# Splitting one expert weight late: w1 stays float32 on chip and is split per block, attention splits w2 alone

## The reference, cut to what matters

```python
x = x + tanh(g_xattn) * xattn(layernorm(x), ctx, ctx)        # 16 heads of 64, context of 64 rows
xt = layernorm(x)                                            # (4096, 256)
w_topk, sel = top_k(xt @ gate_w.T, 2); w_topk = softmax(w_topk)
h = silu(einsum('td,edf->tef', xt, w1))                      # w1 (8, 256, 1024)
y = einsum('tef,efd->ted', h, w2)                            # w2 (8, 1024, 256)
x = x + tanh(g_ffn) * einsum('ted,te->td', y, combine)
```

## Time and profile before

| | |
|---|---|
| median of 3 runs | 850.42 us (848.83 to 853.76) |
| profiled execution, first to last instruction | 848.8 us |
| TensorE, VectorE busy | 769.0 us (91%), 661.1 us (78%) |
| ScalarE, GpSimd busy | 409.8 us (48%), 472.4 us (56%) |
| bytes moved by DMA | 92.52 MB, mean 109 GB/s |

### The profile page before, as it was taken

How to read it: one execution, slowest core, us unless ns; L and a number is a source line. 1 busy time by engine, 2 the same in 40 slices (tenths; PEclk the granted TensorE clock), 3 DMA queues, 4 the chain that set the end, 5 groups by cost and what they waited for, 6 DMA issues and landing times. The chain is left out here.

```text
span 848.8 us, 23770 instructions
## 1 busy us (share of the span) xinstructions
PE 769.0 (91%) x8130; PEld 623.5 (73%) x8131; DVE 661.1 (78%) x1330; ACT 409.8 (48%) x767; POOL 472.4 (56%) x446
## 2 busy tenths in 40 slices
PE   3978998988988888998789999999999999999993
PEld 2645665665655656665578999899999999999993
DVE  7878999999999999999855867766666666666661
ACT  3765776675757667575324444333333333333321
POOL 3434765786868678686633464844444444444442
PEclk9988999999999999999989999999999999999998
DMA  7404061533416153342167786432233332233321
GB/s 237 185 1 149 16 209 51 196 122 144 147 65 230 68 200 99 137 157 93 68 214 212 220 237 159 113 57 45 48 47 46 50 50 46 48 47 46 52 33 19
DMA packets 48837, 92.52 MB, mean 109 GB/s; under 512 B 4921, under 2 KB 32578, under 8 KB 48770
## 3 DMA queue, kind: packets, MB, share of 16 engines
q1 hardware_dynamic: 25730, 64.78, 22.6%
q0 software_dynamic: 13392, 18.03, 12.4%
q10 hardware_dynamic: 9648, 8.85, 3.9%
HBM read 53.69 MB, written 37.95 MB: 108 GB/s over the span
## 5 line engine op out<-in xcount | busy, mean ns | idle before, releaser
L1402 PE MATMUL h_ps<-bx_h,w_now 128*128 128x128 f16 x2272 | 196.1, 220 | 0.6 <-DVE w_now L1538 0.6
L1415 PE MATMUL pair_ps<-weights,ht_h 128*128 x1136 | 190.6, 273 | 0.9 <-ACT y L1481 0.6
L1402 PE MATMUL h_ps<-bx_l,w_now 128*128 128x128 f16 x1136 | 157.1, 220 | 0.0
L1402 PEld LDWEIGHTS h_ps<-bx_h,w_now 128*128 128x128 f16 x2272 | 155.1, 99 | 1.8 <-issue 1.0
L1645 POOL TENSOR_TENSOR wait_mark<-wait_mark 128x1 f32<-128x1 f32 x71 | 50.7, 714 | 189.1 <-ACT y L1481 144.5
L1415 PE MATMUL pair_ps<-weights,ht_l 128*128 x568 | 154.8, 273 | 0.0
L1474 ACT ACTIVATE hid<-h_ps 128x1024 f32<-128x1024 f32 x71 | 72.7, 1024 | 144.2 <-PE h_ps L1402 140.1
L1544 DVE CAST ht_h<-hid 128x1024 f16<-128x1024 f32 x71 | 49.5, 697 | 104.8 <-ACT hid L1474 104.8
L1215 POOL TENSOR_TENSOR r_l<-r,r_h 128x512 f16<-128x512 f32 x64 | 74.9, 1171 | 86.2 <-ACT r_h L804 83.5
L1646 POOL DMA_INDIRECT out<-y,meta x71 | 114.6, 1614 | 14.4 <-issue 6.1
L1415 PEld LDWEIGHTS pair_ps<-weights,ht_h 128*128 128x128 f16 x1136 | 110.2, 97 | 15.9 <-issue 1.7
(11 more groups left out here) (273 smaller groups left out, 1693.8 us busy)
## 6 DMA issues: line engine op xcount, KB each, us to landing
stage<-in_w SPq DMA_DIRECT2D x16, 1024.0 KB, 7.5
w_split<-split SPq DMA_DIRECT2D x14, 1024.0 KB, 5.9
weights<-w_split SPq DMA_DIRECT2D x14, 1024.0 KB
rows<-records ACTq DMA_DIRECT2D x67, 129.0 KB, 2.1
xin<-in_x SPq DMA_DIRECT2D x8, 512.0 KB, 4.2
x_even<-in_x SPq DMA_DIRECT2D x4, 512.0 KB, 3.6
x_odd<-in_x SPq DMA_DIRECT2D x4, 512.0 KB, 3.7
out<-x_even SPq DMA_DIRECT2D x4, 512.0 KB, 2.7
```

The lines of the kernel that those rows point to most:

```text
L1402: last = nc.tensor.matmul(h_ps[r % 2][:, c, :], w1_now[:, r % 2, s, k * F + c * P:k * F + c * P + P], xt[:, r % 2, k, :], start=(j == 0 an ...
L1415: last = nc.tensor.matmul(y_ps[r % 2], ht[:, r % 2, c, :], weights_at(e, s, WN // 2 + c * D, D).rearrange("p o n -> p (o n)"), start=(c == ...
```

## The change

w1 is no longer split in the attention stage. It is loaded as float32 from the input, straight into the place of its expert (8 KB a partition, as many bytes as its two halves had), and each block of the experts stage splits it into `w1_now`: ScalarE multiplies by 64 into the high half (`w1_high`), VectorE makes the low half (`w1_low`), both for block i+2 at the end of step i, in place of the copy `take_w1` of block i+1 at its start. Before block 0 both are done for blocks 0 and 1. Attention splits only w2, in 4 pieces a group: two in step 0, one in step 1, one in step 2 (group 0: two in step 5, two in step 6). `stage` and `split` are half as large, and w_k of the attention has a buffer of its own.

```diff
-WC = 8
+WC = 4
...
+        weights.w2 = nc.alloc_sbuf_tensor_at("weights_w2", [P, E, 2, 2, W2N], F16, offset=nc.sbuf_base)
+        weights.w1 = nc.alloc_sbuf_tensor_at("weights_w1", [P, E, 2, W1N], F32, offset=nc.sbuf_base)
...
         if isinstance(g, int) and g == 0:
-            return range(3 * (p - 5), min(3 * (p - 4), WC)) if p >= 5 else ()
-        return (p,)
+            return {5: (0, 1), 6: (2, 3)}.get(p, ())
+        return {0: (0, 1), 1: (2,), 2: (3,)}.get(p, ())
...
-        def load_w1(e):
-        def load_w2(e):
+        def load_w2(e, half):
+            after(sp, split_lo, WC * e - (WC // 2 if half == 0 else 0))
...
-        load_w1(0)
-        load_w2(0)
+        load_w2(0, 0)
+        load_w2(0, 1)
+        for e in range(HELD):
+            sp.dma_start(weights.w1[:, e, 1, :].rearrange("p (k f) -> p k f", k=KD),
+                         dram["w1"][e].rearrange("(k p) f -> p k f", p=P)).then_inc(w1_held_in, 16)
...
         for e in range(HELD, E):
-            for part in range(LOADS):
-                c = slice(part * WN // LOADS, (part + 1) * WN // LOADS)
-                sp.dma_start(weights[:, e, :, c], dram["w_split"][e][:, :, c]).then_inc(loads, 16)
-                sp.wait_ge(loads, 1 + 16 * ((e - HELD) * LOADS + part + 1))
+            sp.dma_start(weights.w1[:, e, 1, :].rearrange("p (k f) -> p k f", k=KD),
+                         dram["w1"][e].rearrange("(k p) f -> p k f", p=P)).then_inc(loads, 16)
+            sp.wait_ge(loads, 1 + 16 * ((e - HELD) * LOADS + 1))
+            sp.dma_start(weights.w2[:, e, 0], dram["w2_split"][e]).then_inc(loads, 16)
+            sp.wait_ge(loads, 1 + 16 * ((e - HELD) * LOADS + 2))
...
+        def w1_high(i, r):
+
+            e = expert_of(act, i)
+            act.wait_ge(loads, e * (16 * LOADS) + 1)
+            after(act, h_mm, i - 1)
+            nc.scalar.mul(w1_now[:, r % 2, 0, :], w1_at(e), WS).then_inc(w1_hi, 1)
...
             silu(i, r)
+            if there(i + 2):
+                w1_high(i + 2, r)
             if before_now(i - 1):
                 weigh(i - 1, (r - 1) % RB)
+        for i in range(2):
+            w1_high(i, i)
         x_high(0, 0)
...
-        def take_w1(i, r, e=None):
-            nc.vector.tensor_copy(w1_now[:, r % 2], weights[:, bass.ds(e, 1), :, 0:KD * F].rearrange("p o s n -> p (o s) n")).then_inc(w1_ready, 1)
+        def w1_low(i, r):
+
+            e = expert_of(dve, i)
+            dve.wait_ge(w1_hi, i + 1)
+            nc.vector.scalar_tensor_tensor(w1_now[:, r % 2, 1, :], w1_at(e), WS, w1_now[:, r % 2, 0, :],
+                                           ALU.mult, ALU.subtract).then_inc(w1_lo, 1)
...
             if there(i + 1):
-                take_w1(i + 1, (r + 1) % RB)
                 x_low(i + 1, (r + 1) % RB)
             split_h(i, r)
+            if there(i + 2):
+                w1_low(i + 2, r)
...
-        first_expert = expert_of(dve, 0)
+        for i in range(2):
+            w1_low(i, i)
         x_low(0, 0)
-        take_w1(0, 0, first_expert)
```

More of the change, by code:

```diff
@@ L57 @@
 BIG = 3.0e38
-WN = 2 * KD * F
+W1N = KD * F
+W2N = FC * D
 ROUTE = 17
 LAST = 6
-WC = 8
+WC = 4
 def after(eng, sem, count):
@@ L258, in attention @@
     tanhs = sb("tanhs", [P, 2], F32)
-    stage = sb("stage", [P, WN], F32)
-    split = sb("split", [P, 2, WN], F16)
+    stage = sb("stage", [P, W2N], F32)
+    split = sb("split", [P, 2, W2N], F16)
+    wk_sb = sb("wk_sb", [P, W1N], F32)
     ctx_sb = sb("ctx_sb", [P, 2, D], F32)
@@ L306, in attention @@
     ctx_t = x2t[:, :, 0:B // 2 * 3 * M].rearrange("p k (c j m) -> p k c j m", c=B // 2, j=3)
-    wk_sb, wv_sb = (split[:, i, :].bitcast(F32) for i in range(2))
+    wv_sb = split[:, :, :].rearrange("p s n -> p (s n)").bitcast(F32)
     wk_cols = rec[0][:, :, :, :].rearrange("p c t w -> p (c t w)")[:, 0:KD * H * DK].rearrange("p (k n) -> p k n", k=KD)
@@ L448, in store_split @@
             sp.wait_ge(split_lo, done)
-            c = slice(half * WN // 2, (half + 1) * WN // 2)
-            sp.dma_start(at(w_split, e, "o p s n -> (o p) s n")[:, :, c], split[:, :, c]).then_inc(split_stored[half], 16)
+            c = slice(half * W2N // 2, (half + 1) * W2N // 2)
+            sp.dma_start(at(w2_split, e, "o p s n -> (o p) s n")[:, :, c], split[:, :, c]).then_inc(split_stored[half], 16)
         def group(g, par):
@@ L835, in expert_hi @@
                 act.wait_ge(split_stored[half], 16 * (e - HELD))
-            c = slice(i * WN // WC, (i + 1) * WN // WC)
-            dst = weights[:, e] if isinstance(e, int) and e < HELD else split
+            c = slice(i * W2N // WC, (i + 1) * W2N // WC)
+            dst = weights.w2[:, e, 0] if isinstance(e, int) and e < HELD else split
             nc.scalar.mul(dst[:, 0, c], stage[:, c], WS).then_inc(split_hi, 1)
@@ L1319, in experts @@
     loads = sem("weight_loads")
-    xt_mm, x_hi, x_lo, meta_done, w1_ready, h_mm, h_act, h_hi, h_lo, y_mm, y_out, added = (sem(n) for n in (
-        "xt_mm", "x_hi", "x_lo", "meta_done", "w1_ready", "h_mm", "h_act", "h_hi", "h_lo", "y_mm", "y_out", "added"))
+    xt_mm, x_hi, x_lo, meta_done, w1_hi, w1_lo, h_mm, h_act, h_hi, h_lo, y_mm, y_out, added = (sem(n) for n in (
+        "xt_mm", "x_hi", "x_lo", "meta_done", "w1_hi", "w1_lo", "h_mm", "h_act", "h_hi", "h_lo", "y_mm", "y_out", "added"))
     HEAD = 5 * RB
@@ L1351, in expert_of, with w1_at, w2_at @@
         return eng.value_load(table[0:1, i:i + 1] if isinstance(i, int) else table[0:1, bass.ds(i, 1)], min_val=0, max_val=E - 1)
-    def weights_at(e, s, start, n):
-        return weights[:, bass.ds(e, 1), s, start:start + n]
+    def w1_at(e):
+        return weights.w1[:, bass.ds(e, 1), 1, :].rearrange("p o n -> p (o n)")
+    def w2_at(e, s, c):
+        return weights.w2[:, bass.ds(e, 1), 0, s, c * D:(c + 1) * D].rearrange("p o n -> p (o n)")
     def block_loads(i, r):
```

32 lines of the change are left out of this document (14 added, 18 removed).

## The result

The changed kernel takes 861.93 us (median of 4 runs, 860.58 to 862.20) beside 850.59 for the kernel before: a ratio of 1.0124, 95% interval 1.0101 to 1.0148. It is 11.3 us slower; I had forecast 844, faster. The profiled execution has a span of 860.4 us, 11.6 more than before. The kernel before was timed again beside each later set of experiments, at medians of 849.68, 848.44, 850.32, 850.41 and 850.58 us, and the changed kernel only in this first set; so a difference of two medians of different sets is good to some 2 us, and the ratio to the kernel before of the same set is the better measure.

What follows compares the result with a forecast made beforehand. VectorE was taken to bound attention (busy 47.8 of 50 us), TensorE the experts stage. 848.8 - 16.5 (attention) + 10.5 (experts) = 842.8 us for the profiled span; with 1.6 for the median, 844 us, range 837 to 853.

Steps and rivals of the forecast that it cites:

- A removed piece is worth 0.60 us in groups 2 to 6: Attention: VectorE bound there, each removed split saves 0.60 us; 2.4 us a group, 12.0 us over five groups.
- My first rival: Attention gains only half, 8 us, as TensorE becomes the bound; groups of 48.4 us, total time 853 us; chance 0.2.
- VectorE still above 0.93 busy: Attention: sign expected if the forecast held, beside groups of 47.2 us and the stage over near 411.
- 3 more than the start: Early experts: the late first scatter makes block 4 start 8.5 us late, 3 beyond the start's 5.5.
- Steps with routing work come on top: ... about 2 us: Early experts, step 8: the last LayerNorm's shift stands behind w1_low and the placing, ScalarE waits; about 2 us.
- The chain to the first scatter: Early experts: LayerNorm sums end 8.9 us later, so GpSimd's first scatter moves from 446.3 to about 455.2.
- the 2.5 us of slack of a steady block: Experts: VectorE may fall about 2.5 us behind before TensorE waits; said to nearly cover 2.8 in steps 15 to 17.
- The start of the experts: Before the first hidden layer, two blocks of w1 are split first, delaying it from 430.69 to 436.2: +5.5 us.
- Steady blocks: Experts: VectorE's 4.6 us and ScalarE's 3.6 fit in a block of 5.52 us, so no cost, 0 us.
- The second rival: Experts: GpSimd's marks wait for w1_low, the scatter chain sets blocks at 6.1 us, total time 874 us; chance 0.14.
- My third rival: Experts' start costs 5 or 6 us instead of 10.5, total time 839 us; chance 0.16.
- The mark of 0.78 us: Experts: GpSimd's mark at 701.38 beside VectorE's copy, against 0.20 with VectorE idle; cited as showing a wait.

## Why the prediction was wrong

- **A removed piece is worth 0.60 us in groups 2 to 6: this is the step that failed in attention.** 16.5 us were forecast, 8.1 to 8.7 measured. I read VectorE's 47.8 of 50 us as its work and so as the bound. Part of it was waits for GpSimd inside small operations, most of them with two SBUF inputs; the piece's time turned into more of that wait. Up to the first residual, which takes in the plain groups 0 and 1, 4.6 us were gained where I gave 3.2; from there to the residual of group 6, where I gave 12, it was 3.2. My first rival, attention at half the gain, had the right size (8 us), but named TensorE; that its size came out was luck, as it is GpSimd with VectorE's waits for it. One of my signs, VectorE still above 0.93 busy, came true (46.4 of 49.6) although VectorE didn't set the pace: it could not have told the two apart.
- **"3 more than the start" and "Steps with routing work come on top: ... about 2 us": these terms failed in the experts.** The first 20 blocks cost 14.3 us, not 5. The chain to the first scatter was right: it came 9.0 us later counted from the stage's start, 8.9 forecast. But I took its landing to be 6.0 us as before, and with an issue of 3.50 us it was 7.2; and then TensorE ran at the lower clock, which I had priced at nothing; it costs 1.7 us each time. So block 4 was 6.3 us later than the start alone explains, not 3. (0.9 of it came back by block 8.) At block 9 the shift behind w1_low and the placing cost 4.0 us, not 2. From there to block 20 it was another 4.9 where I gave nothing: 1.0 at block 10, in which the clock was low again, 2.0 at block 14, where VectorE waits for a landing, 2.0 in blocks 15 to 20, where VectorE works nearly all the time. I had set the 2.5 us of slack of a steady block against that.
- **The start of the experts: 5.5 forecast, 5.4 measured**, and 2.6 of it gone when block 1's split was moved (2.3 by my terms).
- **Steady blocks: 0 forecast, 0 measured**, over 50 blocks. w1_low and w1_high had the forecast durations. The second rival, in which the scatter chain sets the block, fell as argued: the marks grew from 0.80 to 1.20 us in the mean, and GpSimd's idle time before them shrank from 2.9 to 2.3.
- My third rival, a start that costs little, fell with the two terms above.
- The Trainium skill (SBUF — State Buffer, section "SBUF: two separate sides") bears on both halves: a VectorE operation with two SBUF inputs and a GpSimd operation that reads SBUF can't run at once. I weighed it for w1_low in the steady blocks, where it changes nothing, and not in attention, where VectorE is the one that waits. The runs agree with it: 2.84 us for four elements a partition, 3.50 us against 1.64 for a scatter. The mark of 0.78 us with which I backed it stood beside a copy, which has one input, so that row said nothing of two. It is not the whole cause: in the first blocks it is 4 to 8 of 14 to 16.5 us, and in attention its share is open.

## What to carry to other kernels

A high busy share is no proof that an engine is the bound: look for operations far longer than the same shape takes elsewhere (2.84 us against 0.16 here), and see which engine's operation ends when they end. Before pricing removed work at its duration, ask what the engine would do a moment earlier; shortening the neighbour's work instead shows whether the pace is set there. Work that costs nothing in a steady loop must be priced again in the steps ahead of it, where the slack is already spent, the first transfers are waited for, and a gap of TensorE can take its clock down (here behind two of three).

## What I had not expected of the hardware

- An indirect scatter's issue on GpSimd takes 3.50 us beside a two-input VectorE operation of 2.29 us, 2.43 when that operation comes in two halves, and 1.64 beside four one-input operations of 2.47 us together.
- A VectorE operation of 4 elements a partition waited out three GpSimd operations in a row, 2.84 us, and didn't get in between them.
- After TensorE had been idle from 452.1 to 455.1 us, the granted clock stayed at 1.00 when work began, fell to its lower level 1.2 us later, and was back at 1.00 from 459.7 on.
